# Splitting row maxima in one pass per half, and moving merges, the next rows' normalisation and its transpose in a two-layer attention pipeline

## The reference

```python
x = x + _L0_attn_ref(_layernorm(x), ...)                 # window of +-32 keys, 16 heads of 16
x = x + _L0_xattn_ref(ctx, ctx, _layernorm(x), pad, ...) # 77 keys, a padding mask
x = x + _L0_ffn_ref(_layernorm(x), ...)                  # 8 experts, the best 2 of each row
x = x + _L1_attn_ref(_layernorm(x), ...)                 # causal
x = x + _L1_xattn_ref(_layernorm(x), ctx, ctx, mask, ...)
x = x + _L1_ffn_ref(_layernorm(x), ...)                  # quantised, gated
```

## Time and profile before

| | us |
|---|---|
| median of 3 runs | 2122.26 (2119.05 to 2122.82) |
| the profiled execution | 2117.94 |
| its span | 2116.1 |
| first program, window steps | 18.4 a step |
| first program, wide steps | 13.4 to 15.1 a step |
| experts | about 530 in all |
| second program, narrow steps with merges | 20.7 a step |
| second program, narrow steps without merges | 19.3 a step |
| second program, wide steps | 14.8 a step |

### The profile page before, as it was taken

One profiled execution on the slowest core, in us unless ns is written; L12 is line 12 of the kernel. 1 busy time (PEld: TensorE's weight loads), 2 busy tenths in 40 slices (PEclk: granted clock), 3 DMA queues, 4 the chain that ended last, 5 costly groups with the idle time before them and its releaser, 6 DMA issues. The chain is left out here.

```text
span 2116.1 us, 57339 instructions
## 1 busy us (share of the span) xinstructions
PE 1949.5 (92%) x19802; PEld 1598.6 (76%) x19802; DVE 1256.2 (59%) x5456; ACT 978.8 (46%) x1905; POOL 685.5 (32%) x1244
## 2 busy tenths in 40 slices
PE   7999998999959999999999798899899998999889
PEld 5888886777748999999999577777777775444377
DVE  5788885777541111111115689988778886369964
ACT  2555555666613333333333355555566653357400
POOL 3666664356560000000001554543422320013400
PEclk9999998999969999999999899999999999999999
DMA  7333332334339999999995634433233330000023
GB/s 223 109 112 109 110 128 82 107 108 132 104 117 407 366 345 341 343 339 340 345 342 201 186 119 131 129 121 124 81 103 111 108 113 29 0 0 0 0 68 92
DMA packets 209555, 334.75 MB, mean 158 GB/s; under 512 B 59501, under 2 KB 193426, under 8 KB 200306
## 3 DMA queue, kind: packets, MB, share of 16 engines
q1 hardware_dynamic: 194914, 301.82, 41.4%
q0 software_dynamic: 9552, 26.10, 4.0%
q10 hardware_dynamic: 4928, 4.72, 0.6%
HBM read 193.74 MB, written 28.05 MB: 105 GB/s over the span
## 5 line engine op out<-in xcount | busy, mean ns | idle before, releaser
L2364 ACT ACTIVATE moe_h<-moe_h_ps,moe_weights 128x128 f32<-128x128 f32 x424 | 132.5, 363 | 255.6 <-PE moe_h_ps L2332 226.1
L2797 PE MATMUL ffn_prod_ps<-x_sb,ffn_weights 128*128 128x512 f32 x480 | 210.9, 599 | 7.0 <-ACT ffn_sig_q L2783 7.0
L2396 DVE TENSOR_TENSOR moe_y<-moe_y_ps,moe_weights 128x256 f32<-128x256 f32 x53 | 22.5, 424 | 328.2 <-PE moe_y_ps L2344 328.2
L1398 ACT ACTIVATE causal_prob<-causal_ps 128x768 f32<-128x768 f32 (+1 forms) x192 | 168.7, 878 | 79.3 <-PE causal_ps L1721 79.0
L2275 POOL DMA_DIRECT2D moe_y_dram<-moe_y x71 | 39.4, 554 | 492.5 <-DVE moe_y L2396 484.3
L2332 PE MATMUL moe_h_ps<-moe_h,moe_weights 128*128 128x128 f32 x1696 | 198.1, 275 | 0.0
L2332 PEld LDWEIGHTS moe_h_ps<-moe_h,moe_weights 128*128 128x128 f32 x1696 | 193.6, 192 | 0.1
L2797 PEld LDWEIGHTS ffn_prod_ps<-x_sb,ffn_weights 128*128 128x128 f32 x480 | 91.1, 192 | 124.6 <-issue 110.4
L1071 DVE CUSTOM_DVE_ANT_0 causal_masked<-causal_ps,causal_causal_mask 128x256 bf16<-128x256 f32 (+1 forms) x512 | 151.9, 351 | 32.0 <-PE causal_ps L1687 31.5
L1071 DVE CUSTOM_DVE_ANT_0 window_masked<-window_ps,window_window_mask 128x160 bf16<-128x160 f32 x512 | 135.1, 319 | 45.8 <-PE window_ps L1687 44.6
L1687 PE MATMUL causal_ps<-k_pair,q_pair 64*128 64x78 f32 (+2 forms) x1024 | 101.6, 299 | 35.6 <-DVE causal_m_tok L1071 26.5
(11 more groups left out here) (424 smaller groups left out, 4776.6 us busy)
## 6 DMA issues: line engine op xcount, KB each, us to landing
moe_weights<-moe_w_in SPq DMA_DIRECT2D x53, 2180.0 KB, 9.7
q_pair<-parts SPq DMA_DIRECT2D x512, 128.0 KB
parts<-moe_w_in SPq DMA_DIRECT2D x17, 2180.0 KB, 9.4
k_pair<-parts SPq DMA_DIRECT2D x256, 128.0 KB
k_pair<-parts SPq DMA_DIRECT2D x256, 38.5 KB
moe_y_dram<-moe_y POOLq DMA_DIRECT2D x71, 128.0 KB, 4.0
moe_rows<-moe_slots_dram SPq DMA_DIRECT2D x53, 128.0 KB, 3.8
x_before_ffn_dram<-x_sb SPq DMA_DIRECT2D x16, 256.0 KB, 2.1
```

The costliest lines, as they stand in the source:

```text
L1398: nc.scalar.activation(out, src, ACT.Exp).then_inc(expd, 1)
L2364: nc.scalar.activation(out[:, f, :], psum[:, f // 2, (f % 2) * TM:(f % 2) * TM + TM], ACT.Gelu, bias=bias[:, f:f + 1]).then_inc(done, 1)
L2797: op = nc.tensor.matmul(prod_ps[:, slot, f, :].rearrange("p (b t) -> p b t", b=2), w[:, k, at:at + P], x_cols(n // GROUPS, k), start=(k == ...
```

## The change

Four edits in `attention`:

- `split_max` writes both partition halves with one instruction: one `CAST` and one `TENSOR_TENSOR` of 128 x 16 elements through a strided view (`by_pair`), for two of 128 x 8 each. This holds for narrow and wide steps of both programs.
- From step 3 on, the merges stand behind the row maxima of slots 2, 2, 5 and 7 (`MERGE_AT`) instead of 4, 5, 6 and 7.
- In narrow steps `next_rows` stands at the end of slot 7, behind `row_max` of slot 7 and the last merge, instead of ahead of `row_max` of slot 6. Wide steps keep it ahead of slot 4.
- In slot 0 of narrow steps TensorE calls `turn_normed` behind `shifted` instead of ahead of it. Wide steps are as before.

```diff
+        MERGE_AT = (2, 2, 5, 7)
...
+                def by_pair(cols):
+                    return bass.AP(cols.tensor, cols.offset, [list(cols.ap[0]), [64, 2], [1, 4], [maxw, ST]])
...
-                    cols = m_cols[:, hf].rearrange("p s c -> p c s")
-                    for ab in range(2):
-                        op = nc.vector.tensor_copy(cols[:, 64 * ab:64 * ab + 4, :], m_tok[:, hf, ab])
-                    op.then_inc(m_hi, 1)
+                    both_halves = lambda first: by_pair(m_cols[:, hf, :, first:first + 4])
+                    nc.vector.tensor_copy(both_halves(0), m_tok[:, hf]).then_inc(m_hi, 1)
                     dve.wait_ge(m_hi, n + 1)
-                    for ab in range(2):
-                        op = nc.vector.tensor_tensor(cols[:, 64 * ab + 4:64 * ab + 8, :], m_tok[:, hf, ab],
-                                                     cols[:, 64 * ab:64 * ab + 4, :].bitcast(F32), ALU.subtract)
+                    op = nc.vector.tensor_tensor(both_halves(4), m_tok[:, hf], both_halves(0).bitcast(F32), ALU.subtract)
                     op.then_inc(m_lo, 1)
...
-                        if i == (4 if wide(ref) else 6):
+                        if i == 4 and wide(ref):
                             next_rows(t, ref)
...
-                        if i >= 4 and in_merge(ref, 2):
-                            merge_rows(t + 2, ref + 2, i - 4)
+                        if in_merge(ref, 2):
+                            for n in range(4):
+                                if i == (MERGE_AT[n] if ref >= 3 else n + 4):
+                                    merge_rows(t + 2, ref + 2, n)
+                        if i == 7 and not wide(ref):
+                            next_rows(t, ref)
...
                     if active(ref, 1):
                         scores(t, ref, i)
-                    if i == 0 and now:
-                        turn_normed(t, ref)
...
                     if active(ref, 2):
                         shifted(t, ref, i)
+                    if i == 0 and now:
+                        turn_normed(t, ref)
                     if i == 0 and active(ref, 4):
                         output(t, ref, 0)
```

## The result

The changed kernel takes 2101.81 us (median of 5 runs, 2098.94 to 2106.01) against 2122.26 before; the ratio is 0.9913, with a 95% interval of 0.9894 to 0.9932. A repeat beside other kernels gave 2103.79 against 2122.15, 0.9923 (0.9897 to 0.9949).

The account below looks back on a forecast made before the run. In merge steps VectorE was taken to be on TensorE's path in slots 5 to 7. Merge steps -6.0, narrow steps without merges 0 and wide steps -1.0 summed to -7.0 us: 2115.3 against the median, range 2106 to 2127.

Parts of the forecast that it names:

- The likeliest case: Whole kernel: 7.0 us less, 2115.3 us against the median, own range 2109 to 2120, chance 0.42.
- all of it is won: Merge steps fall to the 19.25 us of steps without merges: 16.7 us less, 2105.6, chance 0.15.
- Slots 4 to 7, -1.10: Merge steps: moving merges and normalising pair off VectorE's path saves 1.10 us, the excess over a step without merges.
- Slots 2 and 3, +0.30: Merge steps: two merges behind slot 2's row maximum cost 0.3 us, the middle between 0 and +0.6 if a gather holds one.
- its 3.3 us: Merge steps: if a gather's port use is writes alone, slots 2 and 3 cost 0 and the sum is 3.3 us lower.
- End of slot 7 and slot 0, +0.25: Merge steps: row maximum 0 starts 1.50 us behind its scores instead of 1.26, costing 0.25; bounds -0.63 and +0.85.
- The lead: Merge steps, slot 0: TensorE's scores come 0.71 us behind the instruction following the row maximum, taken off VectorE's 2.21 us chain.
- Narrow steps without merges, 0: Some 18 steps: the moved normalising pair and shorter split add 0.51 us, just VectorE's wait; 0, range -3.6 to +10.
- slower rival: In 18 narrow steps without merges the split is held 0.56 us longer: +6.3 us in all, 2128.6, chance 0.18.
- a sign of being wrong: Row maximum 0 more than 0.7 us behind its scores in window steps would show the sums for the locks wrong.
- Wide steps, -1.0: First program: the shorter split ahead of row maximum 0 saves 6 x 0.16 = 1.0 us, from 0 to -1.3.
- own first rival: The case of 16.7 us less, 2105.6, with merge steps as short as steps without merges, chance 0.15.

Follow-up runs that it names:

- the kernels above: The changed kernel with the split in four instructions again, 2119.51 us, and the changed kernel itself, 2101.81 us.
- the first four kernels: The kernel before with the late turn only (2118.49 us), the moved merges only (2120.29), the fused split only (2123.03), or moved rows and late turn (2121.00).

## Why the prediction was wrong

The direction was right: merges opened a gap above a step without them, and the changed kernel closes most of it (20.66 to 19.51, against 18.9 to 19.2 for steps 14 and 15 before). That TensorE's own work alone sets the step then is not shown: it is busy for 112.78 of 117.02 us, and in five of eight slots its scores start right behind a row maximum. The likeliest case had 7 us; the profiled executions differ by 16.4. The rival "all of it is won", 16.7 us, at a chance of 0.15, came closest, but its total is in part luck: it is reached with other parts. A merge step gave 1.15 us (20.66 to 19.51) where that rival had 1.43, and ten window steps gave 2.3 where it had nothing.

- **Slots 4 to 7, -1.10.** Measured -1.03. The size was read as the difference to a step without merges, and that it fits so well is in part luck: from step 14 (1461.24 to 1478.03) in place of step 15 it would have been 1.40. The reasons put beside it were partly wrong. The prediction took TensorE's wait list for the path and so put VectorE on it in slots 5 to 7. But slot 4 shrinks by 0.48 with the merges unmoved and the split fused, and grows to 3.19 with the merges moved and the split unfused: the split at slot 3 was on the path too, through row maximum 4. The trace of before shows it, in rows that the prediction did not read, where no wait is listed:

```profile
1387.52 0.46 PE L1687 MATMUL causal_ps<-k_pair,q_pair 64*128 64x256 f32 x1
...
1389.31 0.41 DVE L1071 CUSTOM_DVE_ANT_0 causal_masked<-causal_ps,causal_causal_mask 128x256 bf16<-128x256 f32 x1
...
1390.55 0.45 PE L1687 MATMUL causal_ps<-k_pair,q_pair 64*128 64x256 f32 x4
```

Row maximum 4 starts 1.79 us behind its scores, and slot 5's scores come 1.24 behind its start, as in the kernels above. And none of the single edits keeps the gain of slots 4 to 7.
- **Slots 2 and 3, +0.30: the first term that failed.** Measured +0.03. The prediction took the middle between a merge held by the gather and one that isn't, "as nothing favours an end". The second merge runs at 0.48 in the middle of a gather. The trace of before had such rows, in a filling step of the second program, two merges in their bare time with the first of them wholly inside a gather:

```profile
1180.62 0.87 DVE L1216 SCALAR_TENSOR_TENSOR x_sb<-causal_got,moe_gate,x_sb 128x256 f32<-128x256 f32 x2
...
1180.33 0.96 POOL L790 DMA_INDIRECT moe_got<-moe_y_dram,moe_got_pos  x1 [0.30 <-issue]
```

The Trainium skill, page "SBUF — State Buffer", section "Who interferes with whom", says that an instruction with two SBUF inputs contends with a GpSimd instruction that reads SBUF and not with one that only writes it. On the merge's side the trace agrees, if a gather counts as the second kind: merge 0.48 beside a gather, 0.57 and 0.94 beside a cut, and casts held by both. On the gather's side it does not quite: the gather that starts during the first merge is 0.1 to 0.26 us longer. That is where a cost does arise, and it shows in slot 4 and not in slots 2 and 3: +0.16 with the merges alone. In the changed kernel slot 4 takes 2.56 with the merges in slot 2 and 2.56 with the merges back, so there it is covered. The prediction named the rule with its 3.3 us and took half of the opposite.
- **End of slot 7 and slot 0, +0.25: the second.** Measured -0.11. The chain on VectorE was well sized (2.21 forecast, 1384.44 to 1386.58 is 2.14), with other parts: the pair is held for 1.36 instead of 0.97, and the split behind it is bare. The lead was wrong: 0.71 us from a window step, where the slot 0 scores of a merge step come 1.00 behind the instruction that follows row maximum 7 (1384.44, 1385.44).
- **Narrow steps without merges, 0: the third.** Measured -0.19 in window steps; in the second program steps 14 to 16 together gained nothing. The turn fills TensorE's 0.29 us wait, which the prediction had as the end of its range from below. It also let its slower rival begin where row maximum 0 of a window step is more than 0.63 us behind its scores, "since TensorE has nothing else to do there", and took 0.7 as a sign of being wrong. It is 1.00 behind, and the turn and half a projection are there to do: slot 0 is 0.10 longer than before for it (2.04, 2.14), and slot 1 is 0.28 shorter.
- **Wide steps, -1.0:** measured -1.5.
- **The slower rival** (18 window-like steps held longer) is real and exactly what the fused split prevents: with four instructions row maximum 0 comes 1.39 us behind its scores (252.04, 253.43), TensorE waits 0.27, and the window step takes 18.59, longer than before by 0.16.

With the two positive terms of the merge step at zero and the window steps at the lower end, the prediction's own sum would have been 11 x -1.10 - 3.6 - 1.0 = -16.7. It treated every unknown as a cost to be split in the middle, and its range, down to 2106, left out the lower half of its own first rival. Against the median that sum would have given 2105.6; the measured 2101.81 lies lower still. What of the difference between 16.4 us (traces) and 18 to 20 us (medians) is scatter stays open: single executions of before went from 2109.89 to 2128.35 beside the first four kernels, and the first step of the first program alone took 21.6 to 25.5 us over these kernels, 21.8 in the trace of before and 24.0 in that of the changed kernel.

## What to carry to other kernels

An engine with a queue can be late for several reasons in a row, and then single edits measure as nothing while their union pays in full: the late turn alone gave 0.2%, and the merges, the fusion, and the rows with the turn nothing that could be told, where all together gave 0.8 to 0.9%. So read what a step costs with the whole group gone (here the same step without merges) before judging the parts, and test a group by taking one edit back, not only by putting one in. When an instruction is moved ahead or what stands before it is removed, ask what else it waits for that was hidden, here two GpSimd instructions behind a cut. And a wait list names only idle time: an engine that fills its wait with other work is missing from it, so compare when an instruction starts with the end of what it needs, as for slot 5's scores and row maximum 4.

## What the runs showed of the hardware

- A gather's GpSimd instruction (0.94 to 1.29 us) holds VectorE's casts (0.57 for 0.17) and does not hold a merge of two SBUF inputs: the 31 merges of the changed kernel beside nothing but gathers took 0.47 to 0.50 us, the 7 with nothing beside them 0.47 to 0.48.
- The merges do hold a gather that starts during the first of two: it took 1.14 to 1.29 us in steps 6 to 12 and ended 0.51 behind the second merge each time, where the first gather of a step takes 1.03 to 1.04 beside row maxima. A gather that had started before the merges kept its 0.96 (1180.33). What in the gather waits stays open.
- The fused cast of 128 x 16 takes 0.17 us undisturbed, the two of 128 x 8 that it replaces 0.23 together. Beside GpSimd the fusion saves ten times as much: the split of slot 3 falls from 1.78 to 1.15 us, with two instructions held (0.57 and 0.63) instead of three (0.57, 0.74 and 0.55).
- GpSimd is held in turn: its small addition L53 took 0.37 us at 1373.12, beside a merge, against 0.19 in the kernel with the merges alone, where only row maxima lay beside it.
